# A graph network on one core: GpSimd may gather twelve tiles ahead of TensorE instead of 24

## The chip, the core and the metric

The kernel runs on one core of a Trainium2 chip. Its engines work side by side and meet at semaphores: TensorE (PE in the profile), VectorE (DVE), ScalarE (ACT), GpSimd (POOL) and SyncE (SP), with 16 DMA engines that move data between HBM and the core's memory. The metric is the time of one execution in device microseconds (us); lower is better.

## The reference, cut to what matters

A graph has 3125 nodes with 128 features each and 53125 edges, sorted by destination (17 for each node on average), each of one of eight types. After a layer norm come three relational layers. A fourth layer (not by type) follows after another layer norm, with a two-layer perceptron, a norm over the nodes and a residual.

```python
def rgcn_conv(x, edge_index, edge_type, W, root, bias):
    src, dst = (edge_index[0], edge_index[1])
    out = x @ root + bias
    for r in range(NUM_RELATIONS):
        mask = edge_type == r
        h = x @ W[r]
        msg = jnp.where(mask[:, None], h[src], jnp.zeros((), x.dtype))
        agg = jax.ops.segment_sum(msg, dst, num_segments=N)
        cnt = jax.ops.segment_sum(mask.astype(x.dtype), dst, num_segments=N)
        out = out + agg / jnp.maximum(cnt, 1.0)[:, None]
    return out
...
h = relu(rgcn_conv(h, ..., W1, root1, b1))   # layer 0
h = relu(rgcn_conv(h, ..., W2, root2, b2))   # layer 1
h = relu(rgcn_conv(h, ..., W3, root3, b3))   # layer 2
...
aggr = jax.ops.segment_sum(x[src], dst, num_segments=n)   # the fourth layer
```

## The kernel before, in words

**Tiles.** The edges are cut into 416 tiles (`TILES`) of 128 edges. For each layer a table in HBM (`h_tables`) holds `x @ W[r]` for every node and type. For a tile GpSimd gathers the 128 rows of the table that its edges name into one of the 24 slots (`SLOTS`) of `rows`, by an indirect DMA of 64 KB (`gather`, L1249; the first 11 tiles of layers 1 and 2 at L1269, from the part of the table that is there first). VectorE makes a 128 x 64 selection matrix with the edges' weights (`select`, L962), eight tiles to an announcement, in a ring of 32. TensorE multiplies slot by selection and adds to a sum in PSUM (`sum_tile`, L560): two matmul records for a tile, or four where the tile lies across two sums. The sums of a layer change at tiles 64, 132, 200 and on; each change has eight tiles that lie across it.

**Numbering.** G = 416 x layer + tile. The first 48 tiles (`FORE`) of layer 0 are done in another way, from rows gathered at L1238, so the ring starts with G = 48. The last tile of each layer is not gathered by GpSimd but fetched by SyncE.

**Who waits for whom.** After every fourth tile (`FREE`) TensorE raises `s_mm`. GpSimd asks at every fourth tile (L1265): tile G is gathered only when the tiles up to G-21 are done, so the four after it never get more than 24 ahead. Nothing but gathers stands behind that wait on GpSimd, except at a layer's start, where `wait_table` (L1111 and on) waits for the stored tables. VectorE's `select` waits for `s_mm` too, once in eight tiles, for the tiles up to G-25. `wait_sums` and `fetch_ends` wait for it at a layer's end. A gather tells TensorE by a semaphore of its slot (`s_row`).

**What else runs.** The order of each engine's work is written out by hand, tile by tile. TensorE also makes the next layer's table during layers 0 and 1 (`transform`, L529); ScalarE and VectorE copy it out (`evacuate`, L751) and SyncE stores it (L1082, L1084). In layer 1 TensorE, ScalarE and VectorE build an adjacency matrix for the fourth layer (`pairs` L647, `hots` L844 and L850, `lows` L1047, `add` L1058). In layer 2 TensorE multiplies with it (`dense`, L667), and `turn_back`, `turn_rows` and `products` (L623, L630, L637) close the sums. At tile 12 of layers 1 and 2 `late_sums` (L615) adds, by 64 matmuls, the edges whose sources lie in the last two blocks of nodes.

Of the kernel before, what the change touches and what calls it, by code (L numbers as in the profile page):

```python
# [32 lines left out]
HALO = 64  # L33
SLOTS = 24
BATCH = 8
FREE = 4
SELS = 32
CHUNK = 16
STAGES = 3
# [19 lines left out]
REGS = 16  # L59

FORE = 48
# [28 lines left out]
def gnn_kernel(nc, x, src_t, dst_t, type_t, limits, w_rel, root_w, bias_w,  # L90
# [58 lines left out]
    def stores_of(slot, tables):  # L149

        return slot_of[:tables].count(slot)
# [45 lines left out]

    ENDS = EDGES - P * (TILES - 1)
    END_TILES = [TILES * L + TILES - 1 for L in range(GIN)]
    assert 0 < ENDS <= REGS  # L200

    def gathered(G):

# [19 lines left out]
    with ExitStack() as ctx:  # L223
# [3 lines left out]
        def sem(name):  # L227
            return ctx.enter_context(nc.semaphore(name))
# [198 lines left out]
        s_mm = sem("s_mm")  # L427
# [36 lines left out]
        def wait_sums(eng, L, k, fast):  # L464

            if fast and k == SUMS[L] - 1:
                eng.wait_ge(s_mm, (TILES * (L + 1) - FORE) // FREE)
            elif fast:
# [30 lines left out]
        def table_of(L, b):  # L499

            return BLOCKS * L + b
# [45 lines left out]
        def sum_tile(pe, L, t):  # L547
# [9 lines left out]
            for k, at, in_window, width in pieces(L, t):  # L557
# [5 lines left out]
                if t == last[L][k] and k < SUMS[L] - 1:  # L563
                    mm.then_inc(s_sums, 1)
            if t % FREE == FREE - 1:
                mm.then_inc(s_mm, 1)
# [383 lines left out]
        def select(dve, L, t):  # L950

            G = TILES * L + t
            if t % BATCH == 0:
                if G >= FORE + SELS:
                    dve.wait_ge(s_mm, (G - FORE - SELS + BATCH) // FREE)
                if L == 0:
# [135 lines left out]
        def fetch_ends(sp, L):  # L1092
# [4 lines left out]
            else:  # L1097
                sp.wait_ge(s_mm, (TILES * L - FORE) // FREE)
            for p in range(ENDS):
# [8 lines left out]
        def wait_table(pool, L):  # L1108
            if L == GIN:
                pool.wait_ge(s_xr_out, 16 * SUMS[LAST_REL])  # L1110
                return  # L1111
            for n in range(ALL_STAGES):
                pool.wait_ge(s_stage[n], 32 * stores_of(n, BLOCKS * (L + 1)))
# [100 lines left out]
        @block.gpsimd  # L1214
        def _(pool):
            pool.wait_ge(s_const, 2)
            nc.gpsimd.affine_select(out=wide[:], in_=wide[:], compare_op=ALU.not_equal, fill=1.0, base=0,
                                    pattern=[[-1, 4 * P]], channel_multiplier=1).then_inc(s_pool_const, 1)
            pool.wait_ge(s_const, 6)
            nc.gpsimd.affine_select(out=shift, in_=shift, compare_op=ALU.not_equal, fill=1.0, base=P,  # L1220
                                    pattern=[[-1, 3 * P]], channel_multiplier=1).then_inc(s_pool_const, 1)
            nc.gpsimd.iota(tile_at[:], pattern=[[P, COLS]], base=0, channel_multiplier=0).then_inc(s_pool_const, 1)
            nc.gpsimd.iota(fore_at, pattern=[[REL * FORE_STEP, FORE // BATCH], [REL * STEP, BATCH]], base=-REL * FORE_LEAD,
                           channel_multiplier=0).then_inc(s_pool_const, 1)
            nc.gpsimd.iota(iota_i, pattern=[[1, EARLY + NP]], base=-EARLY, channel_multiplier=0).then_inc(s_pool_const, 1)
            pool.wait_ge(s_src, 32)
            pool.wait_ge(s_x0, 16 * GROUPS)

            beats = itertools.count()

            def pause():
                made = next(beats)
                if made:
                    pool.wait_ge(s_beat, made)
                nc.gpsimd.memset(beat[:], 0.0).then_inc(s_beat, 1)

            for t in range(FORE):
                pool.indirect_dma_start(fore_rows[:, t, :], None, x0_table,  # L1238
                                        bass.IndirectOffsetOnAxis(ap=src_i[:, t:t + 1], axis=0)
                                        ).then_inc(s_fore_row[t // BATCH], 16)  # L1240
                pause()
                pause()
            pool.wait_ge(s_idx, 1)
            pool.wait_ge(s_flag, 1)
            fast = pool.value_load(flag[0:1, 0:1], min_val=0, max_val=1)

            def gather(L, slot, column, landed):
                table = h_tables[L] if L < GIN else xr_table
                pool.indirect_dma_start(rows[:, slot, :], None, table,  # L1249
                                        bass.IndirectOffsetOnAxis(ap=column, axis=0)).then_inc(landed, 16)  # L1250

            with pool.If(fast != 0):
                for L in range(GIN):
                    if L == 0:
                        wait_table(pool, L)
                    else:
                        for n in range(ALL_STAGES):
                            pool.wait_ge(s_stage[n], 32 * stores_of(n, table_of(L, late_blocks[0])))
                        pool.wait_ge(s_late_made, 1)
                    for t in range(0 if L else FORE, TILES):  # L1260
                        G = TILES * L + t
                        if L and t == LATE_TILES:
                            wait_table(pool, L)
                        if G % FREE == 0 and G >= FORE + SLOTS:
                            pool.wait_ge(s_mm, (G + FREE - SLOTS - FORE) // FREE)  # L1265
                        if G in END_TILES:
                            continue
                        if L and t < LATE_TILES:
                            pool.indirect_dma_start(rows[:, G % SLOTS, :], None, h_tables[L][0:REL * NOT_LATE, :],  # L1269
                                                    bass.IndirectOffsetOnAxis(ap=late_idx[:, t:t + 1], axis=0)  # L1270
                                                    ).then_inc(s_row[G % SLOTS], 16)
                        else:
                            gather(L, G % SLOTS, idx[:, t:t + 1], s_row[G % SLOTS])
            with pool.Else():
                pool.wait_ge(g_count, 2)
                for L in range(LAYERS):
                    wait_table(pool, L)
                    with pool.Fori(0, TILES) as t:
                        pool.wait_ge(g_idx, TILES * L + t + 1)
                        pool.sem_inc(g_asked, 1)  # L1280
                        gather(L, 0, col_i[:], g_row)
# [530 lines left out]
```

## Time and profile before

| | |
|---|---|
| median of 3 runs | 1944.0 us (1940.2 to 1953.54) |
| the profiled execution | 1944.79 us |
| its span, from first to last instruction | 1942.9 us |
| TensorE matmul, busy | 1121.3 us, 58% |
| TensorE weight load, busy | 819.6 us, 42% |
| VectorE, busy | 847.5 us, 44% |
| ScalarE, busy | 635.8 us, 33% |
| GpSimd, busy | 1197.7 us, 62% |
| mean granted clock of TensorE | 0.633 of full |

Layer 0's gathers by the ring start at 107.6 us, layer 1's at 653.6 us, layer 2's at 1285.7 us; the last gather starts at 1888.8 us. "Busy" of GpSimd is its own part of a gather, not the transfer. "Idle before" is the time that an engine stood still ahead of an instruction, and what follows the arrow is what ended it: an instruction of another engine, a DMA, "issue" (nothing that the profile shows) or "remote" (a semaphore whose raiser the profile can't name).

### The profile page before, as it was taken

To read this page: it belongs to the slowest core of one execution; us is meant where nothing else is said; L and a number is where in the kernel's file an instruction comes from. 1 tells how busy PE (TensorE), PEld (TensorE's weight loads), DVE (VectorE), ACT (ScalarE), POOL (GpSimd) and SP (SyncE) were. 2 spreads that over 40 slices of the span, in tenths; PEclk is the share of its full clock that TensorE was granted. 3 is DMA by queue.
4 is the path that set the end of the run, shared out by engine and by line. 5 is a ranking of instruction groups with operands and counts; after the bars stand their busy time and mean duration, and the time that the engine had idled before them with its cause. 6 is when DMAs were issued, how large, how long until landed. Compare 5 with 4: busy or idle time off the path is not lost.

```text
span 1942.9 us, 17586 instructions
## 1 busy us (share of the span) xinstructions
PE 1121.3 (58%) x4604; PEld 819.6 (42%) x4627; DVE 847.5 (44%) x3270; ACT 635.8 (33%) x1147; POOL 1197.7 (62%) x1350
## 2 busy tenths in 40 slices
PE   6778655444444655646464656576445564556577
PEld 2256344333434354534343444446333434344445
DVE  4557465455454235656565665661121212122223
ACT  5400500000000247767776766652001111111133
POOL 5755666666666556666666666645666666666650
PEclk9797765555555655656565655665556675766678
DMA  7642333232332311222222222221111111111111
GB/s 227 200 138 80 89 91 102 84 100 81 101 83 84 96 39 45 76 60 71 60 72 63 71 63 60 72 83 40 48 45 47 46 45 46 45 47 46 47 43 35
DMA packets 80802, 144.19 MB, mean 74 GB/s; under 512 B 24687, under 2 KB 38248, under 8 KB 80696
## 3 DMA queue, kind: packets, MB, share of 16 engines
q0 software_dynamic: 39840, 81.67, 17.1%
q1 hardware_dynamic: 40424, 60.68, 9.1%
q8 instruction: 41, 0.67, 0.1%
q10 hardware_dynamic: 432, 0.64, 0.1%
q14 instruction: 65, 0.53, 0.1%
HBM read 100.23 MB, written 42.67 MB: 74 GB/s over the span
## 4 chain that ended last, share of the span: by engine, by line
another core or an unknown queue 28%; PE 25%; issue 21%; DVE 11%; POOL 8%; ACT 6%; DMA 1%; DVEq 1%; SPq 0%; ACTq 0%; POOLq 0%
POOL rows L1249 8%; PE ps_h L529 6%; PE ps_agg L560 6%; DVE early L1058 5%; DVE sel L962 3%; PE ps_a L647 2%; DVE scratch L1047 2%; PE ps_a L667 2%; ACT scratch L844 2%; PE ps_h L667 2%; PE ps_a L578 2%; PE ps_agg L615 1%; ACT stage L816 1%; PE ps_a L601 1%
## 5 line engine op out<-in xcount | busy, mean ns | idle before, releaser
L1249 POOL DMA_INDIRECT rows<-h_table,idx x1175 | 1115.3, 949 | 627.4 <-issue 341.7
L560 PEld LDWEIGHTS ps_agg<-sel,rows 128*128 128x128 f32 x2764 | 590.2, 281 | 328.2 <-issue 269.6
L560 PE MATMUL ps_agg<-sel,rows 128*128 128x64 f32 (+14 forms) x2764 | 581.5, 345 | 212.9 <-issue 171.9
L962 DVE TENSOR_SCALAR sel<-iota,early,norm 128x64 f32<-128x64 f32 x1178 | 356.5, 334 | 427.3 <-remote 281.1
L647 PE MATMUL ps_a<-scratch 128*128 128x300 bf16 x416 | 164.0, 395 | 268.8 <-DVE early L1058 155.0
L1058 DVE TENSOR_TENSOR early<-ps_a,early 128x300 f32 x416 | 195.7, 470 | 270.1 <-remote 203.2
L844 ACT ACTIVATE scratch<-scratch,ones 128x300 bf16<-128x300 f32 x416 | 221.1, 532 | 177.5 <-remote 148.1
L529 PE MATMUL ps_h<-w_all,xT 128*128 128x512 f32 x300 | 206.9, 798 | 119.5 <-ACT xT L756 65.4
L850 ACT ACTIVATE scratch<-iota,code_lo 128x300 f32<-128x300 f32 x416 | 226.5, 545 | 12.5
L940 DVE TENSOR_SCALAR_CACHE_REDUCE agg_s<-scratch,key_f 128x256 bf16<-128x256 int16 x416 | 193.3, 472 | 42.5 <-issue 32.9
L647 PEld LDWEIGHTS ps_a<-scratch 128*128 128x128 bf16 x416 | 59.6, 143 | 309.2 <-issue 296.8
L529 PEld LDWEIGHTS ps_h<-w_all,xT 128*128 128x128 f32 x300 | 62.9, 246 | 162.2 <-issue 69.1
L1047 DVE TENSOR_SCALAR scratch<-iota,code_lo 128x128 bf16<-128x128 f32 x416 | 128.6, 309 | 0.0
L756 ACT ACTIVATE xT<-ps_agg,vecs 128x512 f32<-128x512 f32 (+2 forms) x16 | 9.4, 585 | 291.2 <-remote 280.5
L751 ACT COPY stage<-ps_h 128x512 f32<-128x512 f32 x80 | 46.2, 582 | 173.5 <-remote 102.2
L816 ACT CAST stage<-early 128x3072 bf16<-128x3072 uint8 x13 | 35.7, 2750 | 183.4 <-remote 133.9
L751 DVE COPY stage<-ps_h 128x512 f32<-128x512 f32 x50 | 34.0, 681 | 60.9 <-remote 35.1
L816 ACT CAST w_all<-early 128x3072 bf16<-128x3072 uint8 x12 | 32.9, 2751 | 84.5 <-remote 65.4
L1238 POOL DMA_INDIRECT early<-x_table,early x48 | 45.8, 954 | 23.1 <-DMA x_table<-early 16.4
L763 ACT ACTIVATE hid<-ps_agg,vecs 128x512 f32<-128x512 f32 (+3 forms) x10 | 5.3, 526 | 134.8 <-issue 64.9
L578 PE MATMUL ps_a<-early 128*128 128x384 f32 (+36 forms) x158 | 43.5, 407 | 9.1 <-issue 9.0
L667 PE MATMUL ps_h<-stage,scratch 128*128 128x512 bf16 x96 | 36.6, 477 | 14.7 <-issue 12.2
(158 smaller groups left out, 740.0 us busy)
## 6 DMA issues: line engine op xcount, KB each, us to landing
h_table<-stage SPq DMA_DIRECT2D x130, 256.0 KB
rows<-h_table,idx POOLq DMA_INDIRECT x1175
scratch<-key_rows SPq DMA_DIRECT2D x26, 544.0 KB
h_table<-scratch SPq DMA_DIRECT2D x20, 256.0 KB
x_rows<-in_x SPq DMA_DIRECT2D x6, 256.0 KB, 6.2
w_all<-in_W SPq DMA_DIRECT2D x3, 512.0 KB, 6.6
x_table<-early SPq DMA_DIRECT2D x6, 256.0 KB, 2.3
out<-early SPq DMA_DIRECT2D x6, 256.0 KB
```

Of the source, the lines that this page charges most:

```text
L529: nc.tensor.matmul(half_bank(L, b, half)[:], xT[:, block_of(b)], w_all[:, L, 4 * half:4 * half + 4, :].rearrange("p r o -> p (r o)"), star ...
L560: mm = nc.tensor.matmul(sums_of(L, k)[:, at:at + width], mine, sel[edges, G % SELS, in_window:in_window + width], start=False, stop=(t == ...
L647: nc.tensor.matmul(ps_a[a % A_BANKS][:, 0:HOT], low[:, a % HOTS, :], hot[:, a % HOTS, :], start=True, stop=True).then_inc(s_step, 1)
L667: mm = nc.tensor.matmul(ps_out[q][:], xp[:, b, part, :], fill_of(b)[:, WIDE * q:WIDE * q + WIDE], start=(b == 0 and part == 0), stop=False)
L816: nc.scalar.copy(fill_of(b), adjacency[:, b, 0:SPARE]).then_inc(s_fill, 1)
L844: nc.scalar.activation(hot[:, a % HOTS, :], apart[:, a % 2, :], ACT.Relu, bias=ones[:, 0:1], scale=-1.0).then_inc(s_hot, 1)
L850: nc.scalar.activation(apart[:, a % 2, :], iota[:, EARLY:EARLY + HOT], ACT.Abs, bias=code[:, a:a + 1]).then_inc(s_apart, 1)
L940: done = nc.vector.tensor_scalar(match[:, t % BATCH, :], chunks[:, c % 2, at:at + 2 * P], key_f[:, t:t + 1], 0.0, ALU.is_equal, ALU.add, a ...
L962: done = nc.vector.tensor_scalar(mine, here, dst, weight, ALU.is_equal, ALU.mult)
L1047: nc.vector.tensor_scalar(low[:, a % HOTS, :], iota[:, EARLY:EARLY + P], lo_f[:, a:a + 1], None, ALU.is_equal).then_inc(s_low, 1)
L1058: nc.vector.tensor_tensor(mine, ps_a[a % A_BANKS][:, 0:HOT].rearrange("p (b d) -> p b d", d=REACH), mine, ALU.add).then_inc(s_add, 1)
L1249: pool.indirect_dma_start(rows[:, slot, :], None, table, bass.IndirectOffsetOnAxis(ap=column, axis=0)).then_inc(landed, 16)
```

## The change

`FREE` goes from 4 to 2, and a new constant `AHEAD_OF_PE`, 12, takes the place of `SLOTS` in GpSimd's wait. TensorE raises `s_mm` after every second tile. GpSimd asks at every second tile: tile G is gathered only when the tiles up to G-11 are done, so that it is never more than 12 ahead. The ring keeps its 24 slots, and a tile its slot. The other waits for `s_mm` are written with `FREE` and ask for the same tiles as before.

```diff
-FREE = 4
+FREE = 2
+AHEAD_OF_PE = 12
...
-    assert 0 < ENDS <= REGS
+    assert 0 < ENDS <= REGS and AHEAD_OF_PE <= SLOTS
...
-                        if G % FREE == 0 and G >= FORE + SLOTS:
-                            pool.wait_ge(s_mm, (G + FREE - SLOTS - FORE) // FREE)
+                        if G % FREE == 0 and G >= FORE + AHEAD_OF_PE:
+                            pool.wait_ge(s_mm, (G + FREE - AHEAD_OF_PE - FORE) // FREE)
```

## Rows read from the trace of the kernel before

**Rows 1.** The page's groups: busy us, mean ns, idle us before.

```profile
L1249 POOL DMA_INDIRECT rows<-h_table,idx x1175 | 1115.3, 949 | 627.4 <-issue 341.7
```

**Rows 2.** L1249 by itself in layers 0, 1, 2; waits: us, times.

```profile
L1249 POOL DMA_INDIRECT rows<-h_table,idx x301: 938/944/1126, 199.8 to 629.7; - x151
...
  remote: 55.9, 16
  PE ps_agg L560: 6.2, 3
...
L1249 POOL DMA_INDIRECT rows<-h_table,idx x341: 938/944/1053, 757.7 to 1258.9; - x171
...
  remote: 80.8, 38
...
L1249 POOL DMA_INDIRECT rows<-h_table,idx x301: 938/944/1375, 1450.0 to 1881.3; - x151
...
  remote: 59.4, 19
  PE ps_agg L560: 4.8, 3
```

**Rows 3.** GpSimd in order of time: start us, us, idle before in brackets.

```profile
1017.27 0.94 POOL L1249 DMA_INDIRECT rows<-h_table,idx  x1 [2.03 <-remote]
...
1554.26 0.94 POOL L1249 DMA_INDIRECT rows<-h_table,idx  x1 [0.30 <-issue]
1559.06 0.94 POOL L1249 DMA_INDIRECT rows<-h_table,idx  x1 [3.86 <-remote]
```

**Rows 4.** Groups of GpSimd, 1005.4 to 1015.3 and 1530.3 to 1555.3 us.

```profile
L1249 POOL DMA_INDIRECT rows<-h_table,idx x8 | 7.6, 952 | 4.2 <-issue 2.1 <-remote 2.1
...
L1249 POOL DMA_INDIRECT rows<-h_table,idx x20 | 19.0, 952 | 9.1 <-issue 5.8 <-remote 3.3
```

**Rows 5.** Stretches, GpSimd alone: from:to, us, busy (x gathers), clock, DMA.

```profile
1285.00:1559.00 274.00, 174.12 (x184) 0.57 0.19 48
653.00:1005.40 352.40, 223.84 (x236) 0.57 0.22 60
```

**Rows 6.** Stretches, L560 alone: PE busy (x), weight loads busy (x).

```profile
1307.00:1559.00 252.00, 81.77 (x376) 78.60 (x376) 0.56 0.18 45
660.00:1005.40 345.40, 117.12 (x486) 121.07 (x486) 0.57 0.22 59
```

**Rows 7.** TensorE in order of time, layer 2.

```profile
1551.11 0.26 PE L560 MATMUL ps_agg<-sel,rows 128*128 128x64 f32 x1 [1.86 <-issue]
```

**Rows 8.** Stretches, all engines: PE, PEld, DVE, ACT, POOL busy (x).

```profile
1542.60:1558.80 16.20, 4.29 (x13) 1.84 (x12) 1.89 (x8) 0.00 (x0) 9.55 (x11) 0.65 0.17 45
1559.00:1570.60 11.60, 11.35 (x53) 7.39 (x53) 3.78 (x16) 2.75 (x1) 8.80 (x10) 0.75 0.19 47
```

**Rows 9.** VectorE in order of time, layer 2.

```profile
1558.97 1.88 DVE L962 TENSOR_SCALAR sel<-iota,early,norm 128x64 f32<-128x64 f32 x8 [12.35 <-remote]
```

**Rows 10.** TensorE in order of time, late_sums of layer 2.

```profile
1313.06 3.62 PE L615 MATMUL ps_agg<-scratch,stage 128*128 128x64 f32 x16
...
1318.66 0.28 PE L615 MATMUL ps_agg<-w_all,stage 128*128 128x64 f32 x1 [0.27 <-issue]
...
1339.72 2.60 PE L615 MATMUL ps_agg<-scratch,stage 53*128 53x64 f32 x11 [0.24 <-issue]
```

**Rows 11.** GpSimd in order of time, the same stretch.

```profile
1334.34 0.94 POOL L1249 DMA_INDIRECT rows<-h_table,idx  x1 [0.30 <-issue]
1347.47 0.94 POOL L1249 DMA_INDIRECT rows<-h_table,idx  x1 [12.19 <-PE ps_agg L560]
```

**Rows 12.** The end: GpSimd's last gather in order of time; L560 behind it.

```profile
1888.75 0.94 POOL L1249 DMA_INDIRECT rows<-h_table,idx  x1 [0.30 <-issue]
...
1889.70:1909.00 19.30, 7.40 (x50) 7.66 (x49) 0.82 0.01 3
```

**Rows 13.** The chain that ended last: start us, us, what.

```profile
608.07 2.46 DMA rows<-h_table,idx
```

## The prediction, made blind

> **What bounds the kernel now.** I read the busy shares first: no engine is full, GpSimd at 62% is the fullest. Then the page's groups: the costliest is the gathers, 0.949 us each, with 627 us of idle time on GpSimd before them [rows 1]. So the next view is GpSimd's own line in the steady middle of each layer [rows 2]. From the first to the last start the 300, 340 and 300 steps between those gathers take 429.9, 501.2 and 431.3 us: 1.433, 1.474 and 1.438 us for each tile, in three layers whose other work differs a lot. A gather that waits for nothing takes 0.94 plus 0.30 of idle, 1.25 us [rows 3]. The rest, about 0.2 us a tile, is a few long pauses. They end by "remote" or by TensorE, and in the steady part the only wait that GpSimd has is L1265, for `s_mm`. So **the pauses are the ring limit, 24 tiles ahead, as far as GpSimd has been told of TensorE's progress**.
>
> How long a pause is follows the number of gathers before it. After 8 gathers it was 2.03 us, after 20 it was 3.86 us [rows 3, 4]. Without the usual 0.30 that is 1.73 and 3.56, a line of 0.51 us for each pause and 0.1525 us for each gather.
>
> How far ahead is GpSimd really? Count gathers against matmuls. In layer 1 GpSimd had issued 236 when it paused; TensorE had done 486 matmuls of L560. A tile has two, and four where it straddles two sums (8 tiles at each border, three borders by then), so (486-48)/2 = 219 tiles: 17 ahead [rows 5, 6]. In layer 2, at 1559, it had issued 184, and TensorE, with two borders, (376-32)/2 = 172: only 12 ahead. Tile 184 needs 164 tiles done. Eight tiles' announcements were on their way while GpSimd stood still.
>
> Why late? Before that pause TensorE is slow: single matmuls with up to 1.86 us of idle before them, ended by "issue" and by no wait [rows 7], 13 in 16.2 us against 53 in the 11.6 us after the pause [rows 8]. VectorE, which had waited 12.35 us for the same counter, starts in the same instant as GpSimd [rows 9]. Layer 2's start has it too: the 64 matmuls of L615 begin at full rate (at 1313.06, 16 in 3.62 us), crawl from 1318.66 to 1339.72, and recover 4.4 us after GpSimd's last gather ended at 1335.28 [rows 10, 11]. I read this as: **a long unbroken run of gathers holds up TensorE and its announcements, and a pause of GpSimd sets them free**.
>
> A rule that bears on it: the Trainium skill, NOTIFIC — the notification-queue block, section Overflow: three behaviours, one of which stalls the engine, says that the internal pipeline of the block that writes event records always pushes back on its producers rather than lose one. By that rule the pace follows the number of records per tile, which the change hardly touches, and the 0.51 us for each pause, with the term of 6.1 us that I make of it below, would go. No row here shows such a block; the same page calls a record free for the engine that makes it, so I let neither decide.
>
> **The change, part by part.** All of it is set against the profiled execution: 1944.8 us, of which 1942.9 is span; the median of the runs is 1944.0.
>
> 1. Ring limit 12, asked at every even tile: tile G now needs G-10 done, where a multiple of four needed G-20. In the steady part GpSimd has been at its limit in all three layers, so the wait bites. Queued behind it on GpSimd are only gathers. Longest run without news: 12, not 24. Runs now, steps over waits ended by remote or TensorE: 300/(16+3) = 15.8, 340/38 = 8.9, 300/(19+3) = 13.6 [rows 2]. I put layers 0 and 2 at 12 and leave layer 1, which is below that already. Layer 0 has 367 gathers, 23 pauses now, 31 then; layer 2, behind its first 36, 380 gathers, 28 now, 32 then. Twelve more pauses of 0.51 us: **+6.1 us**. The part that grows with the gathers stays the same in sum. Bounds: no cost at all for a pause (0), and runs of 6 everywhere, 61+63+69 against 23+28+47 pauses, 95 more: +48 us.
> 2. Layer 2's start. GpSimd stops 12 gathers (15 us) earlier, at 1320.3. If TensorE recovers 4.4 us later as before, at 1324.7, it has some 28 of its 64 matmuls done (24 to 1318.66 at 0.226 us each, a few in the crawl); 36 more are 8.1, the first announcements come at 1334.6, and with 12 gathers and one pause of 2.0 net tile 36 goes out at 1351.7, against 1347.47: **+4.2 us**. TensorE is meanwhile 13 us earlier, with half the rows ready. Bounds: 15 us later, when nothing recovers earlier; 13 us earlier, when TensorE decides. Layer 1's start is alike in form, but its 64 matmuls did not crawl, and GpSimd stays 17 ahead for the whole layer, so nothing is lost there.
> 3. The end. GpSimd's last gather starts at 1888.75; TensorE then has 50 matmuls of L560 (one border: 17 tiles) to 1909.0, 19.3 us or 1.14 us a tile [rows 12]. With ten tiles behind, seven fewer: -8.0 us, if GpSimd sets this stretch; nothing, if TensorE does. I take half, **-4 us**.
> 4. Announcing every second tile: 300 more increments, on matmuls that exist, and 300 more waits, on gathers that exist. A satisfied wait leaves the gather's idle time at 0.30 [rows 3]. Zero; if each cost 0.01 us, 3 us. VectorE's wait and the ends of layers ask for the same tiles as before, in other units. The cover is the queue in front of TensorE, which has the rows of at least a few tiles.
> 5. The landing. A gather that TensorE waited for took 2.46 us from issue to landing [rows 13], while 10 to 12 tiles ahead are 12 us or more. This hides it, if TensorE's lead is real and not merely untold.
>
> Sum: 1944.8 + 6.1 + 4.2 - 4 = **1951 us**, no change that can be told. A measurement of this kernel tells about 1% from none, 19 us.
>
> **Rival 1, slower: TensorE runs dry in the pauses.** Place: layers 0 and 2. If the eight late tiles stay eight, GpSimd stops with 12-8 = 4 tiles really ahead, 4.6 us of TensorE's work at 1.14. The pause after 12 gathers (2.6 us) and the landing (2.46) are 5.1: 0.5 us dry, in 63 pauses +31 us, 1982 us. It decides from the point where fewer than five tiles are left when GpSimd stops; if the lateness shrinks with the run (8 x 12/20 = 5, seven left) it costs nothing. For it: at full rate TensorE eats tiles faster than 1.14 us, and layer 0 has waits for rows already. Against: in layer 1 only three tiles are untold. The upper bound of part 1 is the same side: 1945 + 48 + 4, 1997 us.
>
> **Rival 2, faster: a shorter leash frees TensorE.** The crawl begins late in a run of gathers; runs of 12 may end before it. TensorE then leaves layer 2's start 13 us earlier and keeps that, the end gives its whole 8, and layer 1 goes at layer 0's pace, 340 x 0.041 = 14 us: -35, 1910 us. For it: every crawl ends with a pause. Against: the pauses' length per gather is the same line whether TensorE is loaded or not, which looks like a debt of the gathers that must be paid anyway.
>
> **Rival 3: the limit does nothing**, since where TensorE is at GpSimd's heels it is never asked. The counts of 17 and 12, and pauses in all layers, speak against it; it gives 1945 and lies within the forecast.
>
> **How the numbers follow.** Forecast with rival 3: 0.42. Rival 1 with its bound: 0.30. Rival 2: 0.28. The range takes in rival 2's 1910 with some 5 for part 2's earlier end, and rival 1's upper 1997 with part 4's 3: 1905 to 2000. The forecast's own range is 1930 to 1963. Outside it all lie the case that nearly every pause's growing part vanishes, and the case of runs of four.
>
> **What will show it.** Right: 0.51 + 0.15 n still fits the pauses, runs of 8 to 12, paces of 1.44 to 1.48 in all three layers, TensorE's L560 idle for landings no more than now. Part 2: GpSimd stops near 1320 and L615's crawl is over by 1325. Part 3: ten tiles or fewer left behind the last gather. Wrong, slower: more than 38 pauses beyond the present number, or idle of TensorE put down to rows. Wrong, faster: no stretches of single matmuls with 1 to 2 us of "issue" before each, and a pace under 1.42.

## The result, and the profile after

The change made the kernel faster, where the forecast was 1951 us and no change that can be told: 1915.13 us median of four runs (1909.86 to 1917.36) against 1948.35 us of the kernel before beside it (1940.2 to 1953.54), ratio 0.985 with an interval of 0.9813 to 0.9886. Two repeats gave 0.9867 (0.9816 to 0.9918) and 0.9828 (0.9791 to 0.9865). The profiled execution took 1917.36 us with a span of 1915.3, 27.6 us less than the span before. Every line of the kernel is one number higher after the change (L1250 is the gather, L561 the matmul of a tile, L616 `late_sums`).

Two of the page's groups, with busy us, mean ns and idle us before:

```profile
L1250 POOL DMA_INDIRECT rows<-h_table,idx x1175 | 1118.7, 952 | 631.2 <-issue 323.8
L561 PE MATMUL ps_agg<-sel,rows 128*128 128x64 f32 (+14 forms) x2764 | 664.8, 362 | 280.2 <-DMA rows<-h_table,idx 210.3
```

The gathers idle as long as before [rows 1]. The gathers of the three steady stretches, answering to [rows 2], with us and times of the idle time before them:

```profile
L1250 POOL DMA_INDIRECT rows<-h_table,idx x301: 942/947/1114, 199.1 to 629.3; - x151
...
  PE ps_agg L561: 32.6, 16
  remote: 28.9, 17
...
L1250 POOL DMA_INDIRECT rows<-h_table,idx x341: 942/947/1046, 755.1 to 1255.3; - x171
...
  remote: 83.7, 42
  PE ps_agg L561: 3.1, 3
...
L1250 POOL DMA_INDIRECT rows<-h_table,idx x301: 939/947/1367, 1430.0 to 1861.8; - x151
...
  remote: 44.0, 20
  PE ps_agg L561: 23.2, 19
```

The 940 steps took 430.2, 500.2 and 431.8 us, 1362.2 together; before it was 1362.4. **The pace of the gathers (the time from one tile to the next) did not move at all**, so the gain lies outside the steady stretches.

**Nor are these pauses waits for tiles that TensorE has yet to do**, as the prediction's name for them, "the ring limit", suggests. I count idle times over 0.6 us before a gather. Every one in the steady stretches stands where GpSimd asks, but the last matmul of the tile that it asks for had ended before the pause began in 74 of 76 pauses before the change (at the median 4.4 us earlier) and in all 92 after it (6.2 us). In layer 2 after the change, tile 52 asks for tile 41. Here is tile 41 on TensorE, and then tile 52's gather:

```profile
1336.09 0.69 PE L561 MATMUL ps_agg<-sel,rows 128*128 128x64 f32 x2 [0.63 <-DMA rows<-h_table,idx]
...
1348.98 0.95 POOL L1250 DMA_INDIRECT rows<-h_table,idx  x1 [2.11 <-remote]
```

What comes late is the news. The trace keeps the updates of `s_mm`. Before the change it has 260 of 300, and half of them are dated over 2.7 us behind the end of the latest matmul that raises it; GpSimd went on within 0.35 us of such an update in 73 of the 76 pauses. Whether the updates themselves are late, or whatever makes them late holds GpSimd as well, these traces don't separate.

Cutting the span at the starts of the gathers and at TensorE's last tile of a layer shows where (us):

| stretch | before | after | difference |
|---|---|---|---|
| start to layer 1's first gather | 653.6 | 648.2 | -5.4 |
| to layer 1's last gather | 612.8 | 616.5 | +3.7 |
| from there to TensorE's last tile | 26.3 | 11.0 | -15.3 |
| to layer 2's last gather | 596.1 | 596.6 | +0.5 |
| from there to TensorE's last tile | 20.3 | 7.5 | -12.8 |
| the rest | 33.9 | 35.6 | +1.7 |

I call the third and the fifth stretch the **drain**: what TensorE still has to do when GpSimd has started its last gather. A layer cannot end before it is over, and the next layer's table is finished at about the same time: layer 2's first gather started 7.0 us before the drain's end before the change, 5.8 us after it. Layer 0 has a drain too, inside the table's first stretch, of 13.5 us before and 4.2 us after. GpSimd before the change, in order of time, with the idle time in brackets:

```profile
1266.37 0.94 POOL L1249 DMA_INDIRECT rows<-h_table,idx  x1 [0.30 <-issue]
1285.74 0.95 POOL L1269 DMA_INDIRECT rows<-h_table,late  x1 [18.43 <-DMA h_table<-stage]
```

And after:

```profile
1264.72 0.94 POOL L1250 DMA_INDIRECT rows<-h_table,idx  x1 [1.66 <-PE ps_agg L561]
1269.89 0.94 POOL L1270 DMA_INDIRECT rows<-h_table,late  x1 [4.23 <-DMA h_table<-stage]
...
1306.72 0.95 POOL L1250 DMA_INDIRECT rows<-h_table,idx  x1 [0.30 <-issue]
1312.12 0.94 POOL L1250 DMA_INDIRECT rows<-h_table,idx  x1 [4.45 <-PE ps_agg L561]
...
1872.33 0.95 POOL L1250 DMA_INDIRECT rows<-h_table,idx  x1 [2.12 <-PE ps_agg L561]
```

GpSimd's wait for layer 2's table shrank from 18.43 to 4.23 us. How many tiles lay behind the last gather is told by the matmuls of the tile sums. Before, in stretches for L560 alone (us, PE busy with count, weight loads busy with count, clock, DMA):

```profile
1267.30:1292.70 25.40, 10.56 (x56) 10.90 (x56) 0.70 0.23 79
```

After, for L561, answering to [rows 5, 6] at 1005.9 and to [rows 12] at the end:

```profile
651.00:1005.90 354.90, 122.91 (x508) 127.50 (x509) 0.58 0.23 63
...
1265.60:1275.70 10.10, 6.15 (x31) 6.07 (x30) 0.66 0.34 113
1873.20:1879.80 6.60, 3.24 (x24) 3.35 (x24) 1.00 0.04 10
```

At layer 1's end 56 matmuls (20 tiles) became 31 (ten tiles; tiles 404 to 411 lie across two sums and have four each); at the end 50 (17 tiles) became 24 (8 tiles). In the middle of layer 1, (508 - 48) / 2 = 230 tiles were done when GpSimd had issued 238: 8 ahead, where it had been 17.

**Why was TensorE behind at all?** It falls behind in the first run of gathers of each layer. There it crawls: its instructions come one by one, with idle time between them that no wait explains. [Rows 10] showed it in layer 2. After the change the same 64 matmuls, TensorE in order of time:

```profile
1297.18 3.62 PE L616 MATMUL ps_agg<-scratch,stage 128*128 128x64 f32 x16
1300.61 3.60 PE L616 MATMUL ps_agg<-w_all,stage 128*128 128x64 f32 x16
1304.14 3.67 PE L616 MATMUL ps_agg<-scratch,stage 53*128 53x64 f32 x16
1307.63 3.60 PE L616 MATMUL ps_agg<-w_all,stage 53*128 53x64 f32 x16
1311.16 2.18 PE L561 MATMUL ps_agg<-sel,rows 128*128 128x64 f32 x9
```

No crawl: 14 us instead of 33. Layer 1's start has it too, in another form, which I had not looked for. Before the change:

```profile
672.47 0.41 PE L647 MATMUL ps_a<-scratch 128*128 128x300 bf16 x1 [2.99 <-issue]
...
689.37 0.41 PE L647 MATMUL ps_a<-scratch 128*128 128x300 bf16 x1 [7.70 <-issue]
```

Between these two stands one more, at 680.94: one tile in 8.4 us, for as long as GpSimd's first 28 gathers ran (from 653.6 to 688.4); from 693.8 the tiles come 0.8 us apart. After the change GpSimd first pauses at 668, and the tiles come 0.8 us apart from 674.7. Layer 0's start is alike: TensorE crawls from 131.2 to 147, when GpSimd's first run ends at 144.8; after the change the crawl is over at 136.1, with the run at 134. The table has when TensorE had ended a tile, in us after the layer's first ring gather, with the layer's limit at its start:

| kernel | limit at starts | layer 0, tile 60, 104 | layer 1, tile 16, 68 | layer 2, tile 16, 36 |
|---|---|---|---|---|
| before | 24 | 47, 120 | 58, 131 | 62, 70 |
| the change | 12 | 31, 103 | 45, 119 | 43, 61 |
| twelve_in_layer_2 | 24, 24, 12 | 49, 121 | 63, 139 | 42, 59 |
| free2_ahead24_2 | 24 | 50, 121 | 63, 139 | 61, 70 |
| free4_ahead12_2 | 12 | 39, 102 | 43, 117 | 42, 60 |
| ahead16 | 16 | 39, 111 | 48, 125 | 45, 57 |
| ahead8 | 8 | 30, 99 | 40, 115 | 39, 61 |

So TensorE comes out of each layer's start 9 to 19 us sooner, while GpSimd stands where it stood (tile 104 gathered after 92 and 89 us, layer 1's tile 68 after 104 and 107, layer 2's tile 36 after 62 and 57). From there both go at the gathers' pace. In layer 1 the lag that TensorE has at the start is there at the end, as the drain: 17 tiles at tile 68 and 18 at tile 414. In layers 0 and 2 it rises and falls between 2 and 19 tiles.

The rows themselves are not late. Before and after the change, the packets of a gather end 2.2 us after its start (median), but TensorE takes the tile 22.4 us after that start before the change and 6.4 us after it (medians).

### The profile page after: what moved, and what is told of

It is laid out like the page before. It is cut to its first block, busy times and chain, and to the rows that moved or that the text cites. A ratio compares the mean times of both kernels' runs of the same rounds, so it can differ in the third digit from the quotient of the medians.

```text
span 1915.3 us, 17586 instructions
## 1 busy us (share of the span) xinstructions
PE 1209.7 (63%) x4604; PEld 856.7 (45%) x4627; DVE 843.3 (44%) x3270; ACT 636.2 (33%) x1147; POOL 1201.2 (63%) x1350
## 4 chain that ended last, share of the span: by engine, by line
another core or an unknown queue 29%; PE 25%; issue 15%; POOL 14%; DVE 7%; ACT 6%; DMA 2%; DVEq 0%; SPq 0%; ACTq 0%; POOLq 0%
POOL rows L1250 14%; PE ps_agg L561 7%; PE ps_h L530 6%; PE ps_a L648 4%; DVE early L1059 3%; ACT scratch L845 3%; DMA rows<-h_table,idx 2%; DVE sel L963 2%; PE ps_agg L616 1%; PE ps_a L579 1%; DVE scratch L1048 1%; PE ps_a L668 1%; PE ps_h L668 1%; ACT early L1337 1%
## 5 line engine op out<-in xcount | busy, mean ns | idle before, releaser
L1250 POOL DMA_INDIRECT rows<-h_table,idx x1175 | 1118.7, 952 | 631.2 <-issue 323.8
L561 PE MATMUL ps_agg<-sel,rows 128*128 128x64 f32 (+14 forms) x2764 | 664.8, 362 | 280.2 <-DMA rows<-h_table,idx 210.3
L561 PEld LDWEIGHTS ps_agg<-sel,rows 128*128 128x128 f32 x2764 | 625.2, 287 | 459.3 <-DMA rows<-h_table,idx 245.6
L530 PE MATMUL ps_h<-w_all,xT 128*128 128x512 f32 x300 | 220.7, 849 | 59.7 <-issue 24.1
L530 PEld LDWEIGHTS ps_h<-w_all,xT 128*128 128x128 f32 x300 | 67.5, 262 | 101.3 <-issue 62.3
L752 DVE COPY stage<-ps_h 128x512 f32<-128x512 f32 x50 | 34.2, 683 | 100.7 <-remote 85.2
L1239 POOL DMA_INDIRECT early<-x_table,early x48 | 45.7, 953 | 22.8 <-DMA x_table<-early 16.2
L668 PE MATMUL ps_a<-stage,scratch 128*128 128x512 bf16 x108 | 40.9, 494 | 4.4 <-issue 4.4
L539 PE MATMUL ps_agg<-xT,w_all 128*128 128x512 f32 (+3 forms) x52 | 34.7, 763 | 11.0 <-issue 4.8
```

The lines of the kernel that those rows point to most:

```text
L530: nc.tensor.matmul(half_bank(L, b, half)[:], xT[:, block_of(b)], w_all[:, L, 4 * half:4 * half + 4, :].rearrange("p r o -> p (r o)"), star ...
L561: mm = nc.tensor.matmul(sums_of(L, k)[:, at:at + width], mine, sel[edges, G % SELS, in_window:in_window + width], start=False, stop=(t == ...
L668: mm = nc.tensor.matmul(ps_out[q][:], xp[:, b, part, :], fill_of(b)[:, WIDE * q:WIDE * q + WIDE], start=(b == 0 and part == 0), stop=False)
L752: copy(stage_of(H)[:, 512 * half:512 * half + 512], half_bank(L, b, half)[:]).then_inc((s_evA, s_evD)[half], 1)
L1250: pool.indirect_dma_start(rows[:, slot, :], None, table, bass.IndirectOffsetOnAxis(ap=column, axis=0)).then_inc(landed, 16)
```

## The experiments

Two paces came up. In one group of runs the kernel before took 1628 us, and every trace of the group has a tile each 1.25 us and no pauses in the steady stretches; in all the other groups it took 1927 to 1948 us, with 1.43 to 1.47 us and pauses, as in the profile that the prediction rests on. Ratios are to the kernel before in the same group, and only kernels of one pace are compared.

The traces of the two paces differ in one more thing. A gather's landing makes 16 events, 19152 for the 1197 gathers into the ring. The four traces at 1.25 us hold 19137 to 19149 of them; the sixteen at 1.45 us hold 3378 to 5217. In these, an idle time put to "issue" can be a wait whose end was not recorded, unless the kernel has no wait at that place (it has none between the 64 matmuls of `late_sums`). And at 1.25 us an update of `s_mm` is dated 0.01 us (median) behind the matmul that raises it. Whether the load of event records makes the second pace, or both have one cause, no run tells; every time here is that of an execution with a profiled span.

**Where tiles come at 1.25 us.** The announcements alone, `AHEAD_OF_PE = 24`:

> Theory (the shorter limit pays where a layer drains: TensorE trails GpSimd by fewer tiles when GpSimd's gathers of the layer end; the pace of 1.43 to 1.47 us a tile is the gathers' own): with 24 ahead the finer announcements alone change nothing, ratio to the kernel before 0.995 to 1.005, TensorE still ends layer 1 about 26 us after GpSimd's last gather of it. Rival A (the finer announcements bring it, since TensorE and VectorE and GpSimd are told sooner): 0.985, as with the whole change. Rival B (shorter runs of gathers free TensorE from its crawls all along): also about 1.00 here, crawls as long as before.

1628.0 us against 1628.18, ratio 1.0002 (0.9992 to 1.0011). A stretch of layer 1, GpSimd alone:

```profile
670.00:1069.00 399.00, 301.78 (x320) 0.64 0.28 80
```

320 gathers in 399 us, 1.25 each; the long pauses are gone, and TensorE is two or three tiles behind. Part 4's zero holds here. Nor does TensorE crawl, though of the 1197 gathers into the ring only the first has over 0.6 us of idle time before it: the 64 matmuls of layer 2 take 14.1 us. The first and the last 16:

```profile
1090.18 3.62 PE L616 MATMUL ps_agg<-scratch,stage 128*128 128x64 f32 x16
...
1100.63 3.60 PE L616 MATMUL ps_agg<-w_all,stage 53*128 53x64 f32 x16
```

**An unbroken run of gathers does not hold up TensorE by itself**; it does so only at the slower pace.

The limit alone, `FREE = 4`:

> Theory: the limit of 12 alone, announced by fours, brings nearly the whole gain: 0.985 to 0.99. Rival A (the announcements): 1.00. Rival B: 0.985 to 0.99.

1654.04 us, ratio 1.015 (1.0132 to 1.0169), slower. The first gathers of layer 0:

```profile
128.27 0.94 POOL L1250 DMA_INDIRECT rows<-h_table,idx  x1 [5.40 <-PE ps_agg L561]
139.70 0.94 POOL L1250 DMA_INDIRECT rows<-h_table,idx  x1 [6.74 <-PE ps_agg L561]
```

With 24 these stops are absent. Here GpSimd is the bound from first to last, TensorE is at its heels anyway (drains of 6 and 4 us with both limits), and each stop at a layer's start, while TensorE is busy with other work, is lost for good: layer 0's gathering took 472.6 us against 458.5, layer 1's first 68 tiles 92.2 against 85.2, layer 2's first 36 51.6 against 45.0, 28 us of the 30 between the two spans. The two ends of a layer:

```diff
-if G % FREE == 0 and G >= FORE + AHEAD_OF_PE:
+ahead = 12 if t >= 384 else 24     # short_at_ends
+ahead = 24 if t >= 360 else 12     # long_at_ends
```

> The limit is 24 up to tile 383 of each layer and 12 from tile 384 on, announced by twos. Theory: the drains at the ends of layers 0, 1 and 2 are worth some 5, 15 and 10 us (the differences between the two traces at those places), so 0.985 to 0.99, though the first 384 tiles run as before. Rival B (gain all along): at most a third of it, 0.995.

> The limit is 12 up to tile 359 of each layer and 24 from tile 360 on. Theory: TensorE trails far again when the layers end, so all is lost but the 4 us of layer 2's start: 0.995 to 1.0. Rival B: some 9 tenths of the gain stay, 0.987.

1628.61 us, 1.0002 (0.9992 to 1.0012), and 1647.77, 1.0114 (1.0094 to 1.0134). A cost where the limit is short at the start, none where it is long: the same place.

**Where tiles come at 1.45 us: which part of a layer.** The change as it is, and 24 at the starts only (`ahead = 24 if t < (112 if L == 0 else 40) else 12`):

> The changed kernel once more, beside the kernel before. The comparison that I was shown had both near 1930 us with a pace of 1.43 to 1.47 us for each tile (gathers in runs with pauses of 2 to 4 us); the first four experiments had both near 1630 with 1.25 us for each tile and no pauses at all. Theory (two opposite effects: the limit costs GpSimd gathers where TensorE is held up at a layer's start, and saves TensorE's trailing where the gathers pause): at the pace of 1.25 a ratio of 1.013 to 1.016; at the pace of 1.45 again 0.98 to 0.99. Rival (the change is simply faster, and the first four kernels were slower for their own edits): 0.985 at either pace.

> The limit is 24 up to tile 111 of layer 0 and up to tile 39 of layers 1 and 2, and 12 from there on. Theory: at the pace of 1.25 all 22 us of the loss sit in the three starts, so 0.999 to 1.002; at the pace of 1.45 the gain of the ends stays, 0.98 to 0.99. Rival (the finer waits or the limit cost something all along): at 1.25 half of the loss stays, 1.007.

The change: 1922.0 us, 0.9867. With long starts: 1936.97 us, 0.9958 (0.993 to 0.9987), about 60% of the gain gone, although its drains are short (11.4 and 8.6 us). (The trace is that of the slowest of ten executions, 15 us above their median, and shows the loss too large.) TensorE crawls again (layer 1's tile 16 after 76 us), and GpSimd stops. Its stops at tiles 11 and 36 of layer 1, and there is a third of 7.37 us at tile 40, where the limit falls:

```profile
688.70 0.94 POOL L1250 DMA_INDIRECT rows<-h_table,idx  x1 [17.33 <-issue]
732.64 0.94 POOL L1250 DMA_INDIRECT rows<-h_table,idx  x1 [12.33 <-PE ps_agg L561]
```

Layer 1's first 68 tiles took 127.8 us there, 110.9 in the change beside it. The first of these stops is not the limit's: at tile 11 GpSimd waits for the whole table (`wait_table`), and the table is late because TensorE ended layer 0 late. With the short limit at layer 0's end GpSimd goes on into layer 1 1.25 us after its last gather, where it stood idle for 10.4 us before the change; with the long one at layer 1's start its run then goes on through TensorE's last tiles of layer 0. TensorE crawls there too: layer 0's drain is 23.1 us, against 13.5 before the change and 11.7 in the change beside it. Neither the kernel before nor the changed one has this combination, so the loss is not the crawl of a layer's start alone.

> The kernel with 24 up to tile 383 of each layer and 12 from 384 on, again. At the pace of 1.25: 1.000, as it was. At the pace of 1.45, if it comes up: theory 0.985 to 0.99 (the drains at the layers' ends); rival (gain all along) 0.995.

> The kernel with 12 up to tile 359 of each layer and 24 from 360 on, again. At the pace of 1.25: 1.011, as it was. At the pace of 1.45, if it comes up: theory 0.995 to 1.0; rival 0.987.

Short at the ends: 1943.48 us, 0.9983 (0.9959 to 1.0007), nothing gained, with drains of 11.4 and 6.2 us. Its GpSimd at tile 384 of layer 1:

```profile
1241.96 0.95 POOL L1250 DMA_INDIRECT rows<-h_table,idx  x1 [8.64 <-PE ps_agg L561]
```

The drain is short, and GpSimd pays for it by stopping: layer 1's gathers behind tile 68 took 519.6 us, 512.8 in the change and 508.6 before it. That is 11 of the 25 us that layer 1's gathers took more than before the change; the other 14 lie before tile 68, from the same combination of limits as above (layer 0's drain is 22.8 us, the stop at tile 11 16.02 us). So **a short drain alone is the sign of the gain and not its cause**; it must come with a TensorE that did not fall behind. Long at the ends: 1950.36 us, 1.0016 (0.9984 to 1.0048), all of the gain gone, with drains of 24.8 and 18.8. Here the starts are short and TensorE is early. But by the layer's end it is behind again (18 tiles at tile 384 of layer 1): GpSimd, let go, makes a long run, and TensorE falls behind in it, from 8 tiles at tile 359 to 20 at tile 380. The short limit must hold to the end as well.

**How short.** `AHEAD_OF_PE` at 8 and 16:

> The changed kernel with a limit of 8. Theory now (where the gathers go at 1.45 us a tile by themselves, TensorE follows at the same pace with the lead that the layer's start left, and that lead is paid at each drain; where they go at 1.25 without pauses, each tile less of limit costs GpSimd 1.25 us at each layer's start): at 1.45, four tiles less of trailing at two drains, 0.980; at 1.25, 1.03. Rival (TensorE runs dry in the pauses, below some limit): at 1.45 above 0.99, with TensorE idle for landings.

> The changed kernel with a limit of 16. Theory: at 1.45, two thirds of the gain, 0.990 to 0.993; at 1.25, 1.007 to 1.009. Rival (a threshold near 12): at 1.45 1.000 or 0.985.

1915.69 us, 0.9862 (0.9808 to 0.9917), and 1918.72, 0.9856 (0.9816 to 0.9896). The drains follow the limit (26.3 and 20.3 us at 24; 18.2 and 15.3 at 16; 11.0 and 7.5 at 12; 7.0 and 6.6 at 8); the medians at 8, 12 and 16 can't be told apart. The paces are 1.446, 1.473, 1.435 at 8 and 1.430, 1.469, 1.439 at 16.

**What sets the pace.** Most of `dense` left out (`range(FULL_OUT if b == 0 and part == 0 else 1)`), so that TensorE has about 350 matmuls less in layer 2:

> The kernel before (limit 24, announced by fours) with the dense products of the fourth layer left out but for one of six banks: TensorE's work beside the tiles in layer 2 nearly goes. Theory (the pace is the gathers' own): layer 2's pace stays at 1.44 us a tile in that condition, 1.25 in the other, and only TensorE's trailing shrinks: ratio 0.99 to 1.00. Rival (TensorE's load sets the pace): layer 2's pace falls from 1.44 towards 1.25, 0.965.

1930.95 us, 0.995 (0.9915 to 0.9985). Its gathers in layer 2:

```profile
L1249 POOL DMA_INDIRECT rows<-h_table,idx x299: 939/946/1120, 1453.1 to 1878.4; - x150
...
  remote: 46.4, 16
  PE ps_agg L560: 15.6, 4
```

425.3 us for 298 steps, 1.427 each: TensorE's load doesn't set the pace. Its gain of 13 us shows in the lag: in layer 2 the 64 matmuls take 23.9 us instead of 33, tile 36 is done after 61 us instead of 70, and the drain is 16.0 us. Next, the kernel before with two tiny memsets behind each ring gather:

```diff
 gather(L, G % SLOTS, idx[:, t:t + 1], s_row[G % SLOTS])
+pause()
+pause()
```

> The kernel before with two small memsets of GpSimd behind each gather of a full table (as between the first 48 gathers, which go at 1.435 us a tile), so that no long run at 1.25 us arises. Theory (each gather makes a debt that is paid at some 1.40 us a gather, in pauses if it is made faster): at 1.45 the pauses of 2 to 4 us go, the pace stays at 1.44 to 1.48, ratio 0.99 to 1.01; at 1.25, 1.13. Rival (the pauses come from the limit and TensorE's lateness, whatever the gathers' spacing): the pauses stay, pace near 1.62, 1.10 or more; at 1.25 also 1.13.

1949.01 us, 1.0033 (1.0001 to 1.0066). GpSimd in order of time, and its gathers in layer 2:

```profile
1602.02 0.95 POOL L1249 DMA_INDIRECT rows<-h_table,idx  x1
1602.97 0.27 POOL L1235 MEMSET beat<- 128x1 f32 x2
```

```profile
L1249 POOL DMA_INDIRECT rows<-h_table,idx x297: 943/946/1329, 1449.2 to 1879.8; - x149
...
  remote: 17.2, 9
  PE ps_agg L560: 3.0, 2
```

A gather starts every 1.36 us (0.94 and the memsets' 0.42), 0.11 more than before, some 33 us in 300; but the pace is 430.6 us for 296 tiles, 1.455, only 5 us more in 300 tiles, and the time put to remote and TensorE fell from 64.2 [rows 2] to 20.2 us. What is taken slowly need not be paused for. In this kernel that reads like a debt, a fixed time that each gather owes, whether it is paid at once or in parts; what is owed, and to what, no run shows. The same with the limit of 12:

> The change, and two small memsets of GpSimd behind every ring gather, as in paced_gathers. If the gathers carry a debt that GpSimd pays either in pauses or spread out, then the two add nothing and spare nothing: the pace stays 1.44 to 1.49 us a tile, the drains are those of the change (11 and 8 to 13 us), ratio to the kernel before 0.985 to 0.99. If what helps in the change is that runs of gathers are short, spacing them should help too and add to it: 0.98 or less. If the memsets are late where GpSimd is the bound (layers' starts): 0.99 to 1.0. In the condition of 1.25 us a tile: 1.03 or more, since a gather then starts every 1.45 us instead of 1.25.

1929.19 us, 0.9945 (0.9922 to 0.9969): worse than the change by two thirds of its gain, though the profiled execution (span 1917.8) shows it less. TensorE is as early as in the change (drains 10.7 and 9.1), and the gathers are slower: 516.3 us behind tile 68 of layer 1 against 509.6. Spacing the gathers doesn't do what the short limit does.

**Limit or announcements.** The two halves of the change again, now at 1.45 us:

> The limit of 12 alone: GpSimd asks every fourth tile, and TensorE announces every fourth (FREE = 4), ahead 12. Theory (the gain is the drain behind each layer's last gather, which scales with how far GpSimd may be ahead): the same gain as the change, -25 to -30 us, ratio 0.985 to 0.99, if the tiles come at 1.43 to 1.47 us with pauses; the drain of layer 1 falls from 26 to about 11 us and that of layer 2 from 20 to about 8. Rival (the announcements by two are what frees TensorE and brings it closer): ratio 0.995 to 1.005, drains at 20 us and over. If the tiles come at 1.25 us without pauses: 1.015 again.

> Announcements and questions by two, limit 24 as before. Theory: nothing, ratio 0.997 to 1.003, drains of 20 us and more behind the last gathers of layers 1 and 2. Rival (announcements by two make the gain): 0.985 to 0.99. If the tiles come at 1.25 us: 1.000.

The limit alone: 1907.23 us, 0.9825 (0.9787 to 0.9862). The announcements alone: 1943.48 us, 1.0013 (0.9988 to 1.0039). The drains of the first (stretches, L561):

```profile
1262.20:1270.20 8.00, 4.89 (x20) 4.86 (x20) 0.53 0.29 88
1867.10:1873.20 6.10, 3.24 (x24) 3.35 (x24) 1.00 0.04 11
```

and of the second, and then its 64 matmuls in order of time:

```profile
1272.10:1296.30 24.20, 11.80 (x61) 12.02 (x61) 0.71 0.24 83
1892.20:1912.30 20.10, 7.69 (x50) 8.22 (x50) 0.83 0.01 3
```

```profile
1320.23 1.90 PE L616 MATMUL ps_agg<-w_all,stage 128*128 128x64 f32 x8
1324.22 0.28 PE L616 MATMUL ps_agg<-w_all,stage 128*128 128x64 f32 x1 [2.09 <-issue]
```

It is the limit that gains, and `FREE` has no part in it that can be told. Limit 12 in layer 2 alone (`ahead = AHEAD_OF_PE if L == 2 else SLOTS`):

> Limit 12 in layer 2 alone, 24 in layers 0 and 1; announcements by two. Theory of the drains: only layer 2's end is gained, 20.3 to 7.5-13.5 us, and layer 2's start (61.7 to 57): -10 to -17 us, ratio 0.991 to 0.995, and layer 1's drain stays at 26 us. Rival (the gain is made in layer 1, by TensorE being 17 us further at its end): 1.000, the drain of layer 2 being limited by TensorE. In the condition of 1.25 us a tile: 1.003 to 1.005.

1932.29 us, 0.9973 (0.9948 to 0.9999), 11 us below free2_ahead24_2, its nearest kin. Layer 2 has the crawl taken out and a drain of 5.6 us, layer 1's drain stays:

```profile
1271.20:1295.40 24.20, 10.71 (x58) 10.85 (x57) 0.71 0.24 83
1890.30:1895.00 4.70, 2.31 (x17) 2.27 (x16) 1.00 0.05 14
```

Each layer gives its own part, by its own start.

**A version that beats both?** With questions by four the limit was tried at 8, beside the change:

> The change as it is, a third time, as the measure for free4_ahead8 on one chip. Expected by all theories: 0.983 to 0.988 where tiles come at 1.45 us, 1.013 to 1.017 where they come at 1.25 us.

> Limit of 8, asked and announced by four: GpSimd may gather tile G only when the tiles up to G-5 are done. Theory of the drains: 1 to 4 us less behind each last gather than with 12 (7 and 7 us against 7 to 11 and 8 to 13), so 0.98 to 0.985, if TensorE does not run dry. Rival (four tiles are too few behind a pause: 2.6 us of pause and 2.46 us of landing are more than TensorE's work on four tiles): the pace goes above 1.48 us a tile and the ratio is 1.0 or more. In the condition of 1.25 us a tile: 1.02 or more.

The change: 1893.1 us, 0.9828 (0.9791 to 0.9865). Limit 8: 1905.24 us, 0.9883 (0.9861 to 0.9905). TensorE doesn't run dry behind the pauses (steady paces 1.433, 1.454 and 1.428), but the starts are longer: layer 2's first 36 tiles 60.0 us against 52.6, layer 1's first 68 109.4 against 104.5, layer 0's gathering 539.8 against 530.3. This looks like the cost that the limit had at 1.25 us a tile, and at 8 by fours it seems to begin to eat the gain (the two intervals, 0.9791 to 0.9865 and 0.9861 to 0.9905, barely meet). The limit of 12 by fours, at 0.9825, is level with the change; nothing tried beats it.

## Why the prediction was wrong

**The step that failed** is "nothing is lost there": the sum put TensorE's lag behind GpSimd at nothing in layer 1, halved it at layer 2's end, and left TensorE's start where it was. The runs showed that the lag is paid as the drain of each layer, 15.3 and 12.8 us less with the short limit.

The fullest engine was read rightly, GpSimd with its gathers and their pauses, and so was that TensorE and its announcements are held up in long runs. That the pauses are "the ring limit" was right only in the prediction's own rider, "as far as GpSimd has been told": TensorE's work was done, and the news was late. The mechanism that decided was rival 2, given 0.28, with nearly the right size (1910) and partly the wrong places. The range of 1905 to 2000 holds the measured 1915 only because it took in that rival.

- **Part 1, +6.1 us: nothing.** The runs came out as forecast, 12 in layers 0 and 2 (25 pauses of over 0.6 us in each steady stretch, where there had been 18 and 19; the prediction counted 19 and 22 waits, short ones among them) and 8 in layer 1 (42, before 39). These are means: the longest run in the changed kernel is 28 gathers (layer 2's tiles 24 to 51), and TensorE stayed two tiles behind it without a crawl. But 16 more pauses cost -0.2 us. The fixed 0.51 us for each pause was an artefact: the line went through a pause behind 8 gathers in layer 1 and one behind 20 in layer 2, and the two layers differ. Within a layer the pause less 0.30 is in proportion to its run: in layer 2 2.91 us behind 15.8 gathers before and 2.21 behind 12.0 after, 0.184 each both times; in layer 1 1.91 behind 8.7 and 1.74 behind 8.1, 0.22 and 0.215. paced_gathers shows the same from another side. The prediction used the reading "a debt of the gathers" against rival 2 and did not apply it to its own sum.
- **Part 2, +4.2 us: -4.4.** GpSimd stopped at 1307.7, and TensorE didn't first crawl and then recover: it had not begun to crawl. In the kernel before it began when 12 gathers of the run from tile 11 to tile 35 were out; in the changed one the whole run was 12 gathers, tiles 12 to 23. The failing step was to leave TensorE's start where it was and move only GpSimd's stop.
- **"Nothing is lost there", of layer 1's start: wrong**, and the largest miss of the sum. Its 64 matmuls did run at full rate, as the prediction says, but the tiles before them came 8.4 us apart. A lead of 17 tiles for a whole layer was taken to be harmless. It is a lag of TensorE, and a lag is paid at the layer's barrier: 26.3 us of drain, of which 15.3 went, a term that the sum did not have.
- **Part 3, -4 us: -12.8.** TensorE had 8 tiles behind the last gather, as forecast (ten or fewer), and the whole difference counts, at more than 1.14 us a tile. Halving it had no row behind it; the 8.0 us were themselves too few, since nine tiles fell away and the clock in the drain was 1.00 against 0.82 [rows 12].
- **Part 4, 0: confirmed**, 1.0013 and 1.0002 for the announcements alone.
- **Part 5, and rival 1.** Rival 1 didn't happen, but the sign that the prediction gave for it did: TensorE's idle time put to rows. For the weight loads and matmuls of layer 2's tiles (us, times), before:

```profile
  issue: 177.2, 173
  DMA rows<-h_table,idx: 18.5, 30
```

  and after:

```profile
  DMA rows<-h_table,idx: 212.1, 294
  issue: 106.9, 146
```

  Most landings' events are missing in both traces, so these are lower bounds; but the share is the same (3543 and 3542 of 19152). TensorE now waits for rows at GpSimd's heels, where it was held back before, and the pace is GpSimd's in both. Idle time of an engine that isn't the bound was the wrong sign to name.
- **Rival 2's 14 us from layer 1's pace** did not come (1.474 to 1.471). Layer 1 gave 15.3 us by its drain. Layer 2's start and end were counted as 13 + 8 and gave 4.4 + 12.8 (less 3.9 in the gathers between them): they are one gain, made at the start and seen at the end.
- **The rule that was weighed** (the Trainium skill, NOTIFIC — the notification-queue block, section Overflow: three behaviours, one of which stalls the engine), that the block which writes event records pushes back on its producers: by it the pace follows the records per tile, and the pace did stay, at every limit. That agrees and doesn't show it. The events missing from the traces at 1.45 us, and the late updates, would fit a load on the path of these records, though by the page the block's own pipeline loses none; where they were lost isn't shown. Leaving out 350 matmuls (no_dense) moved layer 2's pace by 0.011 us, and no run here shows the block.

Shown by runs: the limit, not the announcements; that it must be short in the middle and at the end, and that a long one at the starts costs (with the combination named above); each layer for itself; a pace that no limit moves. Argued from traces only: that long runs of gathers are what holds up TensorE at the pace of 1.45 us. The rows agree in three layers and in every kernel of the table; but at 1.25 us longer runs hold up nothing, one run of 28 held up nothing at 1.45 us, and a pause without a limit at the same place was not tried. Why the gathers seem to owe anything, why the news of TensorE is late, and why neither is so when tiles come at 1.25 us, stays open.

## What to carry to other kernels

A producer that is far ahead for a whole stage isn't a reserve: look at the stage's end, count what the consumer still has to do there, and follow that lag back to where it arose, often a burst at the stage's start. A shorter limit is worth it where the burst itself slows the consumer, and costs where the producer is the bound and is stopped at the starts; both happened in this kernel, -1.5% and +1.5%. A price per event must be fitted from events of one stage. And a pause at a wait isn't yet a wait for work: compare the end of what is asked for with the pause's start.

## What the runs showed of the hardware

- The same kernel took 1628 us in one group of runs and 1927 to 1948 us in the others; the group of 1628 us and one at 1946 us ran on the chip of the same number, so it isn't a matter of the chip alone. A gather of 128 rows by GpSimd starts every 1.25 us in a run at either pace (0.94 + 0.30); the difference comes up as pauses, 0.18 to 0.22 us for each tile.
- At the pace of 1.45 us, while GpSimd issued 25 to 28 gathers in a row, single instructions of TensorE (weight loads counted) were up to 2.1 us apart in layer 2 and a chain over three engines slowed to 8.4 us a tile in layer 1. With a limit of 12 neither lasted. At the pace of 1.25 us GpSimd gathered whole layers without a pause, and the same 64 matmuls took 14.1 us.
- At 1.45 us TensorE's semaphore updates are dated late (by over 2.7 us for half of those recorded before the change) and 18 to 27% of the gathers' landing events are in the trace; at 1.25 us the updates are dated 0.01 us behind the matmul, and all but 3 to 15 of 19152 events are there.
- A gather of 64 KB ends its packets 2.2 us after its start, at either pace.
- The mean granted clock doesn't tell the two kernels apart: 0.633 of full before and after.
